# Softmax probabilities of a 256-key window packed into two key tiles, and the work moved with them

## The chip, the cores and the metric

One Trainium2 chip, one core. The metric is device time of one execution in microseconds (us), median of three runs.

## The reference, cut to what matters

Two layers over 2048 tokens of width 512 (two sequences of 1024), all in float32. Layer 0 is a linear recurrence (`W_in`, 32 decays, an associative scan, `W_out`) and a SwiGLU whose weights are rounded to three values. Layer 1 is attention with a sliding window and a mixture of experts (8 experts of width 352, two for each token, and a shared expert of width 1408). Around each of the four parts stands `x = x + layernorm(part(layernorm(x)))`. The part that the change is about:

```python
q, k = apply_rope(rms_norm(q, q_scale)), apply_rope(rms_norm(k, k_scale))   # 16 query heads, 8 key heads, width 128
mask = (j <= i) & (i - j < 256)                                # i: query, j: key
logits = where(mask, (q * ATTN_SCALE) @ k.T, finfo.min)
probs = softmax(logits)
enc = probs @ v
y = einsum('btnh,nhd->btd', enc, out_kernel)
```

The router of the experts is `logits = x @ router_weight.T`, softmax, the two largest; beside it stands a sigmoid gate of the shared expert. These ten columns are called the router products below.

## The kernel before, in words

The work is one program per engine; semaphores tie them. Each engine's order is written out by hand, call by call, and engines wait only where a call waits on a semaphore. Matrix products are made in passes of a faster float format: each operand is kept as a high and a low part (`_hi`, `_lo`), and a product is hi*hi + hi*lo + lo*hi (`passes`, L307), so nearly every value that TensorE uses is first copied to `_hi` by ACT and subtracted to `_lo` by DVE or POOL.

The phases in order of time are: the recurrence, the ternary SwiGLU (to about 430 us), attention (about 400 to 1335 us), its norm (to 1352 us), and, after a barrier, the experts (to the end). The last group of the SwiGLU overlaps the first tiles of attention, and the last head of attention overlaps the norm, whose code is `BlockNorm`.

Attention runs over 8 key heads `k` (each with 2 query heads, `GRP = 2`), and in a head over 16 tiles of 128 tokens (8 for each sequence). For a tile `j` (counted through as `m`):

- `project` (PE): 12 products into `ps_x`; `qkv_out`, `squares`, `split_v` (ACT), `rms`, `rope_add`, `split_v` (POOL), `rope` (DVE);
- `turn` (PE): 3 transposes of q and k; `split_qk` (ACT, then DVE);
- `scores` (PE, L3212): both query heads against the last `ktiles` = min(j % 8, 2) + 1 key tiles. 12 of 16 tiles have three; they are called full tiles here. Six products of 384 columns into `ps_s`;
- `row_max` (DVE, L1587): for each query head one fused instruction adds the mask, writes the masked scores to `pr` in SBUF and takes the maximum; then a tiny one (`nb`, L1597) scales it;
- `exps` (ACT, L2450): two exponentials of 384 columns in place in `pr`, with their sums; `inverse` (DVE); `weigh` (POOL, L952): two multiplications by the inverse;
- `turn_p` (PE, L3223): the probabilities are transposed, six 128x128 pieces of a full tile, into `ps_pt`, which has one buffer;
- `split_p`: `pT_hi` by ACT (L2444), `pT_lo` by DVE (L1628), 768 columns in a full tile;
- `weigh_v` (PE, L3233): nine products of 256 columns; `split_e` (ACT, DVE); `project_out` (PE): six products of 512; `sum_out` (DVE).

In the whole kernel that makes 96 full tiles, 16 with two key tiles and 16 with one. Heads 1 to 6 run the same written order; head 0 and head 7 have their own. A tile's steps are spread over some three tile times, since PE works on other tiles in between.

The norm behind attention handles each tile twice: a mean and variance (DVE), a reciprocal root (POOL), a normalization (ACT); POOL adds to x between the two halves. With `small=True` POOL makes three small instructions for each half (`_rstd_shift`, L147 to L151).

In the experts' phase, `acc` has four PSUM banks. Its PE program begins (L4336) with the router products of four blocks of 512 tokens, 8 products each; then come the shared expert's first chunks. The first weights of the shared expert (`sraw_gu`) are loaded by SP after the barrier, split by ACT and DVE.

Of the kernel before, what the change touches and what calls it, by code (L numbers as in the profile page):

```python
# [314 lines left out]
class Swiglu:  # L315
# [65 lines left out]
    def tern_op(self, dve, dst, src, w, tern_no, done):  # L381
# [159 lines left out]
NL = 10  # L541
POST_SEMS = ("y_stat", "y_rstd", "y_shift", "y_normed", "x_new", "x_stat", "x_rstd", "x_normed", "turned", "xT_hi",
# [15 lines left out]
def mixers_phase(nc, io, keep):  # L558
# [6 lines left out]
    with ExitStack() as ctx:  # L565
# [23 lines left out]
        ps_xp, ps_dd, ps_out, ps_t = ps("xp", [P, 2, BLK]), ps("dd", [P, 2, BLK]), ps("out", [P, 2, D]), ps("t", [P, 2, D])  # L589
# [16 lines left out]
        att_place = {"q_hi": 0, "q_lo": 2, "rot": 4, "pr": 8, "mask": 14, "pT_hi": 16, "pT_lo": 19, "o_lo": 22, "v_lo": 26,  # L606
# [5 lines left out]
        def aa(n, shape, dt=F32):  # L612
# [8 lines left out]
        mask = aa("mask", [P, WT * P])  # L621
# [7 lines left out]
        pr = aa("pr", [P, 2, GRP, WT * P])  # L629
        mx, nb_, sm, ri = sb("mx", [P, 2, GRP]), sb("nb", [P, 2, GRP]), sb("sm", [P, 2, GRP]), sb("ri", [P, 2, GRP])  # L630
        pT_hi, pT_lo = aa("pT_hi", [P, WT, GRP, P], F32R), aa("pT_lo", [P, WT, GRP, P], F32R)
# [3 lines left out]
        ps_pt = ps_out[:].rearrange("p a (b g t) -> p (a b) g t", b=2, g=GRP)  # L635
# [3 lines left out]
                         io["x_mid"], io["x_mid"], lambda dve, n: dve.wait_ge(sa("acc"), NT * (KVH - 1) + n + 1), tag="att_n", share=pre, small=True)  # L639

        def ktiles(i):
            return min(i % BT, WT - 1) + 1

# [18 lines left out]
        def _(sp):  # L662
# [108 lines left out]
            f.norm.tile_store(sp, 2)  # L771
            f.norm.tile_store(sp, 3)
            f.norm.tile_load(sp, 6)
            f.norm.tile_load(sp, 7)
            f.norm.tile_store(sp, 4)
            f.norm.tile_store(sp, 5)
            f.norm.tile_store(sp, 6)
            f.norm.tile_load(sp, 8)
            f.norm.tile_store(sp, 7)
            f.norm.tile_load(sp, 9)  # L780
# [3 lines left out]
            f.norm.tile_store(sp, 9)  # L784
            f.norm.tile_store(sp, 10)
            f.norm.tile_load(sp, 12)
            f.norm.tile_store(sp, 11)
            f.norm.tile_load(sp, 13)
            f.norm.tile_load(sp, 14)
            sp.wait_ge(s("down"), NT * f.groups)  # L790
# [4 lines left out]
            f.norm.tile_load(sp, 15)  # L795
# [13 lines left out]
            for n in range(NT):  # L809
                norm.tile_store(sp, n)  # L810
                if n + TPB < NT:
# [5 lines left out]
        def _(pool):  # L817
# [134 lines left out]
            def weigh(j, n):  # L952
                w = ktiles(j) * P
                pool.wait_ge(sa("ri"), n + 1)
                pool.nop(nofuse=True)
                for g in range(GRP):
                    p = pr[:, j % 2, g, WT * P - w:WT * P]
                    pool.tensor_scalar(p, p, ri[:, j % 2, g:g + 1], 1.0, ALU.mult, ALU.mult).then_inc(sa("p"), 1)  # L958

# [30 lines left out]
            f.norm.y_rstd_shift(pool, 0, (3,))  # L990
            f.norm.x_add(pool, 0, (3,), True)
            f.norm.x_rstd_shift(pool, 0, (2,))
            f.norm.x_rstd_shift(pool, 0, (3,))
            f.norm.y_rstd_shift(pool, 1, (0,))
            f.norm.x_add(pool, 1, (0,), True)
            f.norm.y_rstd_shift(pool, 1, (1,))
            f.norm.y_rstd_shift(pool, 1, (2,))
            f.norm.x_add(pool, 1, (1,), True)
            f.norm.x_add(pool, 1, (2,), True)
            f.norm.y_rstd_shift(pool, 1, (3,))  # L1000
            f.norm.x_rstd_shift(pool, 1, (0,))
            f.norm.x_add(pool, 1, (3,), True)
            f.norm.x_rstd_shift(pool, 1, (1,))
            f.norm.x_rstd_shift(pool, 1, (2,))
            f.norm.y_rstd_shift(pool, 2, (0,))
            f.norm.x_rstd_shift(pool, 1, (3,))
            f.norm.x_add(pool, 2, (0,), True)
            f.norm.y_rstd_shift(pool, 2, (1,))
            f.norm.x_add(pool, 2, (1,), True)
# [3458 lines left out]
```

## Time and profile before

| what | value |
| --- | --- |
| runs | 2028.62, 2021.69, 2028.62 us; median 2028.62 |
| profiled execution | 2022.66 us, span 2020.8 us |
| PE busy | 96% of the span, 10126 products |
| DVE, ACT, POOL busy | 73%, 59%, 40% |
| mean granted clock of TensorE | 0.989 of full speed |

Products overlap in their pipeline, so the duration of one (274 ns for a 128x128 transpose) is longer than the time from its start to the start of the next. A busy PE is not a PE at its peak; the distance between starts tells what a product costs.

### The profile page before, as it was taken

The page shows a single profiled execution, that of the slowest core. Times are in us where ns is not written, and L with a number is a line of the kernel's source. Part 1 is how long each engine was busy: PE and PEld are TensorE (multiplying, and loading weights), DVE is VectorE, ACT ScalarE, POOL GpSimd, SP SyncE. Part 2 cuts the span into 40 slices and gives each one's busy share as a digit, 9 for nine tenths or more (in the row PEclk, how much of TensorE's full clock was granted, in tenths as well). Part 3 has the DMA queues.
Part 4 walks back from the last instruction along what each step waited for, and adds up shares of the span by engine and source line. Part 5 has one row for each costly group of instructions (what it writes and reads, how often), then busy time and mean ns, then how long its engine had stood idle before and what let it go on. Part 6 is the DMA issues. An engine that isn't in the chain of part 4 may idle for free. (4 is left out here: it accounts for less than half of the span.)

```text
span 2020.8 us, 32102 instructions
## 1 busy us (share of the span) xinstructions
PE 1942.5 (96%) x10126; PEld 1649.1 (82%) x10126; DVE 1479.4 (73%) x3410; ACT 1198.0 (59%) x2977; POOL 802.0 (40%) x1202
## 2 busy tenths in 40 slices
PE   7999999989999999999999999979999999999996
PEld 5677777768888888888888888857788889887875
DVE  7788565687777777777777778966387778774665
ACT  6753222467666666666667667764386677773342
POOL 3342000685655555555555557952400000001452
PEclk9999999999999999999999999989999999999998
DMA  7344010227000000000000100234799899984563
GB/s 268 123 144 139 16 48 21 79 73 240 22 12 22 12 22 12 1 33 1 22 12 22 33 1 8 62 110 148 273 342 305 312 325 313 319 297 146 198 204 109
DMA packets 82518, 245.02 MB, mean 121 GB/s; under 512 B 10784, under 2 KB 11424, under 8 KB 80448
## 3 DMA queue, kind: packets, MB, share of 16 engines
q1 hardware_dynamic: 77232, 226.20, 32.7%
q0 software_dynamic: 5120, 16.78, 2.3%
q8 instruction: 83, 1.36, 0.3%
q14 instruction: 83, 0.68, 0.1%
HBM read 207.55 MB, written 45.61 MB: 125 GB/s over the span
## 5 line engine op out<-in xcount | busy, mean ns | idle before, releaser
L307 PE MATMUL l_xp<-att_w_hi,xT_hi 128*128 128x512 f32 x512 | 207.7, 406 | 5.1 <-ACT att_qkv L2426 4.6
L307 PE MATMUL l_xp<-att_w_hi,xT_lo 128*128 128x512 f32 x512 | 200.5, 392 | 0.0
L307 PE MATMUL l_xp<-att_w_lo,xT_hi 128*128 128x512 f32 x512 | 199.7, 390 | 0.0
L2455 ACT ACTIVATE att_pr<-att_pr,rec_nb,rec_r 128x384 f32<-128x384 f32 (+2 forms) x256 | 168.7, 662 | 36.4 <-DVE rec_nb L1597 35.6
L958 POOL TENSOR_SCALAR att_pr<-att_pr,rec_ri 128x384 f32<-128x384 f32 (+2 forms) x256 | 141.2, 564 | 122.4 <-DVE rec_ri L1626 118.8
L3885 POOL DMA_INDIRECT y<-moe_rows,moe_slotA x16 | 16.4, 1024 | 413.7 <-DMA moe_rows<-moe_lo_f 410.6
L962 POOL TENSOR_TENSOR att_rot<-att_rot,att_rot 128x384 f32<-128x384 f32 x128 | 130.0, 1016 | 107.8 <-DVE att_rot L1620 107.8
L1593 DVE CUSTOM_DVE_ANT_0 att_pr<-l_dd,att_mask 128x384 f32<-128x384 f32 (+2 forms) x256 | 119.1, 501 | 67.0 <-PE l_dd L307 60.9
L2426 ACT ACTIVATE att_qkv<-l_xp 128x512 f32<-128x512 f32 x128 | 76.4, 597 | 120.8 <-PE l_xp L307 112.1
L1631 DVE TENSOR_TENSOR att_pT_lo<-l_out,att_pT_hi 128x768 fp32r<-128x768 f32 (+2 forms) x128 | 108.8, 850 | 27.7 <-ACT att_pT_hi L2448 27.5
L2448 ACT ACTIVATE att_pT_hi<-l_out 128x768 fp32r<-128x768 f32 (+2 forms) x128 | 92.7, 724 | 41.8 <-PE l_out L3229 20.8
L307 PEld LDWEIGHTS l_xp<-att_w_hi,xT_hi 128*128 128x128 f32 x512 | 96.5, 188 | 23.9 <-issue 5.4
L2441 ACT ACTIVATE att_sq<-att_qkv 128x128 f32<-128x128 f32 x384 | 114.1, 303 | 1.3
L950 POOL TENSOR_TENSOR rec_r<-rec_ms,pre_nhalf 128x3 f32<-128x3 f32 x128 | 110.6, 864 | 10.7
L307 PEld LDWEIGHTS l_xp<-att_w_hi,xT_lo 128*128 128x128 f32 x512 | 96.2, 188 | 21.5
L307 PEld LDWEIGHTS l_xp<-att_w_lo,xT_hi 128*128 128x128 f32 x512 | 96.7, 189 | 17.4
L307 PE MATMUL l_t<-att_o_hi,att_e_hi 128*128 128x512 f32 x256 | 104.4, 408 | 1.7 <-DVE att_e_lo L1636 1.7
L307 PE MATMUL l_t<-att_pT_hi,att_v_hi 128*128 128x256 f32 x336 | 101.1, 301 | 0.8 <-DVE att_pT_lo L1631 0.6
L3229 PE MATMUL l_out<-ident,att_pr 128*128 128x128 f32 x672 | 95.4, 274 | 6.3 <-POOL att_pr L958 2.9
L4028 DVE TENSOR_TENSOR moe_rgu_lo<-y,moe_rgu_hi 128x1408 fp32r<-128x1408 f32 x59 | 95.5, 1618 | 7.3 <-ACT moe_rgu_hi L4178 7.3
L307 PE MATMUL l_t<-att_o_lo,att_e_hi 128*128 128x512 f32 x256 | 100.5, 392 | 0.0
L307 PE MATMUL l_t<-att_o_hi,att_e_lo 128*128 128x512 f32 x256 | 100.3, 392 | 0.0
(329 smaller groups left out, 6528.6 us busy)
## 6 DMA issues: line engine op xcount, KB each, us to landing
y<-in_moe_rt SPq DMA_DIRECT2D x59, 704.0 KB, 6.5
y<-in_moe_rt SPq DMA_DIRECT2D x39, 768.0 KB, 6.5
moe_sraw_gu<-in_moe_sgu SPq DMA_DIRECT2D x44, 512.0 KB, 3.7
moe_sraw_d<-in_moe_sd SPq DMA_DIRECT2D x44, 256.0 KB, 4.4
moe_xs<-in_zeros SPq DMA_DIRECT2D x39, 256.0 KB, 6.9
moe_lo_f<-moe_xs SPq DMA_DIRECT2D x39, 256.0 KB, 6.8
moe_rows<-moe_lo_f SPq DMA_DIRECT2D x39, 256.0 KB, 6.7
att_raw_w<-in_qkv_w SPq DMA_DIRECT2D x8, 1024.0 KB, 4.8
```

The source lines that it names most:

```text
L307: mm = pe.matmul(out, lhsT, rhs, start=(i == 0), stop=(i == len(terms) - 1))
L950: pool.tensor_tensor(r[:, i % 4, :], ms[:], pre.nhalf[:, 0:3, 0], ALU.pow).then_inc(sa("r"), 1)
L958: pool.tensor_scalar(p, p, ri[:, j % 2, g:g + 1], 1.0, ALU.mult, ALU.mult).then_inc(sa("p"), 1)
L962: pool.tensor_tensor(rot[:, i % 2, :], rot[:, i % 2, :], rot2[:], ALU.add).then_inc(sa("roped"), 1)
L1593: dve.tensor_tensor_reduce(pr[:, j % 2, g, WT * P - w:WT * P], ps_s[:, g, 0:w], mask[:, WT * P - w:WT * P], 1.0, -3e38, ALU.add, ALU.max, ...
L1631: dve.tensor_tensor(pT_lo[:, 0:w, :, :], ps_pt[:, 0:w, :, :], pT_hi[:, 0:w, :, :].bitcast(F32), ALU.subtract).then_inc(sa("pT_lo"), 1)
L2426: act.activation(qkv[:, i % 2, :], ps_x, ACT.Copy).then_inc(sa("qkv"), 1)
L2441: act.activation(sq[h][:], qkv[:, i % 2, HD * h:HD * (h + 1)], ACT.Square, accum_out=ss[:, h:h + 1]) \
L2448: act.activation(pT_hi[:, 0:w, :, :], ps_pt[:, 0:w, :, :], ACT.Copy).then_inc(sa("pT_hi"), 1)
L2455: act.activation(p, p, ACT.Exp, scale=r[:, j % 4, g:g + 1], bias=nb_[:, j % 2, g:g + 1], accum_out=sm[:, j % 2, g:g + 1]).then_inc(sa("exp ...
L3229: mm = pe.transpose(ps_pt[:, u, g, :], pr[:, j % 2, g, P * (WT - w + u):P * (WT - w + u + 1)], ident[:])
L4028: dve.tensor_tensor(rgu_lo[:, p % 3, :], rraw_gu(p), rgu_hi[:, p % 3, :].bitcast(F32), ALU.subtract) \
```

## The change

In a full tile the oldest key tile counts only where key > query (in the tile) and the newest only where key <= query: the two masks complement each other. The change writes the newest tile's scores over the masked places of the oldest, so that a full tile has 256 columns of scores instead of 384 from the maximum on. After the transposes the packed piece is taken apart again with a triangle of ones (`pA` = packed * triangle, `pC` = packed - pA), and `weigh_v` has nine products as before.

```diff
 def row_max(j, m):                                   # DVE
-    wait(dve, "pturn", m - 1)
-    for g in range(GRP):
-        dve.tensor_tensor_reduce(pr[...], ps_s[:, g, 0:w], mask[...], 1.0, -3e38, ALU.add, ALU.max, mx[...])
+    last = ps_s[:, :, P * (w - 1):P * w]
+    if w == WT:
+        dve.copy_predicated(ps_s[:, :, 0:P], mask[:, 0, :]..., last).then_inc(sa("mx"), 1)
+    else:
+        dve.tensor_tensor(last, last, mask[:, 2, :]..., ALU.add).then_inc(sa("mx"), 1)
+    dve.wait_ge(sa("mx"), 2 * m + 1)
+    dve.reduce_max(mx[:, j % 2, :], ps_s[:, :, 0:packed(j) * P], AX.X).then_inc(sa("mx"), 1)
 def exps(j, m):                                      # ACT
+    wait(act, "pturn", m - 1)
-        act.activation(p, p, ACT.Exp, ...)
+        act.activation(pr[:, j % 2, g, 0:packed(j) * P], ps_s[:, g, 0:packed(j) * P], ACT.Exp, ...)
+def weigh(j, n):                                     # ACT, from tile 9 of head 0 on; POOL before
+    for g in range(GRP):
+        act.activation(p, p, ACT.Copy, scale=ri[:, j % 2, g:g + 1]).then_inc(sa("p"), 1)
 def scores(j, m):                                    # PE
-    wait(pe, "mx", GRP * m)
+    wait(pe, "exp", GRP * m)
 def turn_p(j, m):                                    # PE: packed(j) = min(ktiles(j), 2); ps_pt has two buffers
-    wait(pe, "pT_lo", m)
-    for u in range(w):
+    wait(pe, "pT_lo", m - 1)
+    for u in range(packed(j)):
+def part_a(j, m):                                    # POOL; DVE in head 0 up to tile 7
+    pool.tensor_tensor(pA[:], pT[:, :, 0, :, :], mask[:, 1, :]..., ALU.mult).then_inc(sa("parts"), 1)
+def part_c(j, n):                                    # POOL
+    pool.tensor_tensor(pC[:], pT[:, :, 0, :, :], pA[:], ALU.subtract).then_inc(sa("parts"), 1)
 def weigh_v(j, m):                                   # PE: full tile
+    parts = [(t0 - 1, pT[:, :, 1, :, :], None), (t0 - 2, pA, 1), (t0, pC, 2)]
+    for q, (kt, pp, made) in enumerate(parts):
+        if made:
+            pe.wait_ge(sa("parts"), 2 * full_steps(m) + made)
```

`part_a` and `part_c` are 128x512 each (high and low parts, two query heads); `pT`, `pA` and `pC` have one buffer. The four banks of `acc` are allocated once for both phases, and attention's `ps_out` and `ps_t` lie in them. Further:

```diff
+def router(b):                                       # PE, b = 0, 1, 2, at the end of attention
+    out = (ps_out[:, 0, :], ps_out[:, 1, :], ps_e)[b]
+    passes(pe, out[0:2 * NL, :], [...])              # 8 products
 # experts' phase, PE
-for b in range(NB):
-    passes(pe, acc[b][0:2 * NL, :], [...]).then_inc(s("ps_lg"), 1)
+passes(pe, acc[NB - 1][0:2 * NL, :], [...]).then_inc(s("ps_lg"), 1)
 # SP, behind the norm's tile_store 10
+sp.wait_ge(sa("proj"), NT * KVH)
+sp.dma_start(keep["sraw_gu"][:], io["moe_sgu"][0]).then_inc(sa("sraw"), 16)
+def first_shared():                                  # ACT, in the norm behind attention
+    act.activation(keep["sgu_hi"][:, 0, :], keep["sraw_gu"][:], ACT.Copy)
 # the norm behind attention
-norm = BlockNorm(..., small=True)
+norm = BlockNorm(...)
```

Without `small`, DVE makes the first and the last of the three small instructions of each half norm (`ve`, `sh`), and POOL only the root. Each engine's written order, from the SwiGLU's last group to the end of the norm, is a new one throughout: it has the same calls for the rest, with each `last_turn`, `project` and so on some places earlier or later. In the new last stretch `router(0)` stands behind `last_turn(1, 1)`, `router(1)` behind `last_turn(2, 0)` and `router(2)` behind `last_turn(3, 1)`. In the ternary weights' splits one semaphore increment that nothing waits on is left out.

## Rows read from the trace of the kernel before

**Rows 1.** Stretch; busy us of PE, PEld, DVE, ACT, POOL; PEclk, DMA share, GB/s.
```profile
350.00:500.00 150.00, 135.49 (x685) 112.39 (x686) 117.49 (x292) 93.56 (x249) 99.95 (x179) 0.98 0.41 132
...
600.00:1200.00 600.00, 599.20 (x3458) 528.11 (x3457) 451.80 (x1476) 406.40 (x1404) 338.87 (x533) 1.00 0.05 16
...
1310.00:1352.00 42.00, 29.37 (x163) 23.93 (x161) 34.08 (x74) 28.41 (x52) 30.67 (x63) 0.83 0.36 107
...
1361.00:2021.00 660.00, 634.36 (x3164) 540.66 (x3162) 449.56 (x567) 372.63 (x502) 109.13 (x96) 0.99 0.72 252
```

**Rows 2.** Timeline of PE in head 4: start, duration, line, operation, count.
```profile
1002.33 0.36 PE L307 MATMUL l_t<-att_pT_hi,att_v_hi 128*128 128x256 f32 x1
...
1003.49 0.38 PE L3229 MATMUL l_out<-ident,att_pr 128*128 128x128 f32 x2
...
1006.52 0.60 PE L3229 MATMUL l_out<-ident,att_pr 128*128 128x128 f32 x4
1006.87 0.47 PE L307 MATMUL l_t<-att_o_hi,att_e_hi 128*128 128x512 f32 x1
...
1008.34 0.39 PE L307 MATMUL l_xp<-att_w_hi,xT_hi 128*128 128x512 f32 x1
...
1011.07 0.49 PE L3209 MATMUL l_xp<-ident,att_rot 128*128 128x128 f32 x3
1011.31 0.42 PE L307 MATMUL l_dd<-att_k_hi,att_q_hi 128*128 128x384 f32 x1
...
1012.45 0.82 PE L3229 MATMUL l_out<-ident,att_pr 128*128 128x128 f32 x6
1013.02 0.36 PE L307 MATMUL l_t<-att_pT_hi,att_v_hi 128*128 128x256 f32 x1
```

**Rows 3.** Groups of ACT and DVE by shape, whole span: busy, mean ns, idle before.
```profile
L2455 ACT ACTIVATE att_pr<-att_pr,rec_nb,rec_r 128x384 f32<-128x384 f32 x192 | 134.2, 702 | 26.4 <-DVE rec_nb L1597 25.6
...
L2426 ACT ACTIVATE att_qkv<-l_xp 128x512 f32<-128x512 f32 x128 | 76.4, 597 | 120.8 <-PE l_xp L307 112.1 <-POOL att_v_lo L939 7.0 <-issue 1.1
...
L2455 ACT ACTIVATE att_pr<-att_pr,rec_nb,rec_r 128x256 f32<-128x256 f32 x32 | 18.9, 595 | 0.2 <-DVE rec_nb L1597 0.2
...
L1593 DVE CUSTOM_DVE_ANT_0 att_pr<-l_dd,att_mask 128x384 f32<-128x384 f32 x192 | 98.9, 552 | 53.5 <-PE l_dd L307 49.1 <-PE l_out L3229 4.3
...
L1631 DVE TENSOR_TENSOR att_pT_lo<-l_out,att_pT_hi 128x768 fp32r<-128x768 f32 x96 | 91.2, 950 | 21.9 <-ACT att_pT_hi L2448 21.8
...
L1631 DVE TENSOR_TENSOR att_pT_lo<-l_out,att_pT_hi 128x512 fp32r<-128x512 f32 x16 | 10.8, 677 | 0.0
```

**Rows 4.** Groups of POOL by shape, whole span.
```profile
L962 POOL TENSOR_TENSOR att_rot<-att_rot,att_rot 128x384 f32<-128x384 f32 x128 | 130.0, 1016 | 107.8 <-DVE att_rot L1620 107.8
L958 POOL TENSOR_SCALAR att_pr<-att_pr,rec_ri 128x384 f32<-128x384 f32 x192 | 112.2, 597 | 95.5 <-DVE rec_ri L1626 91.9 <-issue 3.6
L950 POOL TENSOR_TENSOR rec_r<-rec_ms,pre_nhalf 128x3 f32<-128x3 f32 x128 | 110.6, 864 | 10.7
...
L200 POOL TENSOR_TENSOR att_x<-att_x,y 128x512 f32<-128x512 f32 x16 | 20.6, 1287 | 0.2 <-ACT y L184 0.2
```

**Rows 5.** Timeline from the norm to the experts, PE and ACT: the router products.
```profile
1352.20 0.59 PE L307 MATMUL moe_acc<-xT_hi,rw 128*20 128x512 f32 x1 [3.15 <-PEq L40]
...
1355.25 0.40 PE L307 MATMUL moe_acc<-xT_hi,rw 128*20 128x512 f32 x1
...
1360.81 0.40 PE L307 MATMUL moe_ps_g<-xT_hi,moe_sgu_hi 128*128 128x512 f32 x1
...
1355.86 1.06 ACT L4147 ACTIVATE moe_sgu_hi<-moe_sraw_gu 128x1024 fp32r<-128x1024 f32 x1 [6.16 <-DMA moe_sraw_gu<-in_moe_sgu]
```

**Rows 6.** Rotated q and k (att_rot) alone, same stretch: PE, PEld, DVE, POOL busy.
```profile
600.00:1200.00 600.00, 42.27 (x258) 32.83 (x258) 138.53 (x510) 87.47 (x86) 1.00 0.05 16
```

**Rows 7.** Timeline in head 0: POOL and DVE at the same time.
```profile
437.66 2.58 POOL L935 TENSOR_TENSOR att_o_lo<-att_raw_o,att_o_hi 128x1024 fp32r<-128x1024 f32 x1
437.91 2.48 DVE L1613 SCALAR_TENSOR_TENSOR att_rot<-att_qkv,rec_r,att_tab 128x128 f32<-128x128 f32 x1
```

More of the change, by code:

```diff
@@ L1219, in _ @@
+            rms(10, 122)
+            rope_add(9, 121)
+            split_v(9, 121)
+            norm.x_rstd(pool, 0, (1,))
+            split_v(10, 122)
+            norm.y_rstd(pool, 0, (3,))
+            part_a(6, 118)
+            norm.x_add(pool, 0, (2,), True)
+            part_c(6, 118)
             rope_add(10, 122)
             rms(11, 123)
-            weigh(8, 120)
+            norm.y_rstd(pool, 1, (0,))
+            norm.x_rstd(pool, 0, (2,))
             split_v(11, 123)
-            norm.x_add(pool, 1, (0,), True)
@@ L1237, in _ @@
+            part_a(7, 119)
+            rms(12, 124)
+            part_c(7, 119)
+            rope_add(11, 123)
+            split_v(12, 124)
+            norm.x_rstd(pool, 0, (3,))
+            norm.y_rstd(pool, 1, (1,))
+            norm.x_add(pool, 1, (0,), True)
+            rms(13, 125)
+            rope_add(12, 124)
+            norm.y_rstd(pool, 1, (2,))
             rope_add(13, 125)
             rms(14, 126)
[L1239 removed]
             split_v(13, 125)
[L1241 removed]
@@ L3372, in _ @@
+            scores(8, 8)
             turn(9, 9)
-            turn_p(5, 5)
-            project_out(0, 4, 4)
-            scores(8, 8)
-            weigh_v(5, 5)
-            turn_p(6, 6)
+            weigh_v(6, 6)
             project_out(0, 5, 5)
-            weigh_v(6, 6)
-            turn_p(7, 7)
-            turn(10, 10)
             project(0, 12, 12)
             scores(9, 9)
+            turn(10, 10)
+            project(0, 13, 13)
+            turn_p(8, 8)
             weigh_v(7, 7)
-            turn_p(8, 8)
@@ L3386, in _ @@
-            project(0, 13, 13)
             project_out(0, 6, 6)
+            scores(10, 10)
+            turn_p(9, 9)
             turn(11, 11)
-            scores(10, 10)
             weigh_v(8, 8)
-            turn_p(9, 9)
+            project_out(0, 7, 7)
             project(0, 14, 14)
@@ L3540, in _ @@
+            turn_p(2, 114)
             project_out(6, 15, 111)
             project(7, 6, 118)
-            turn_p(2, 114)
+            weigh_v(1, 113)
+            scores(3, 115)
+            turn(4, 116)
+            project_out(7, 0, 112)
+            project(7, 7, 119)
             scores(4, 116)
-            weigh_v(1, 113)
+            turn_p(3, 115)
+            weigh_v(2, 114)
             turn(5, 117)
-            project(7, 7, 119)
-            project_out(7, 0, 112)
+            project_out(7, 1, 113)
@@ L3571, in _ @@
-            project(7, 11, 123)
-            project_out(7, 5, 117)
-            scores(9, 121)
-            turn_p(7, 119)
-            weigh_v(6, 118)
-            turn(10, 122)
-            project(7, 12, 124)
+            weigh_v(5, 117)
+            project(7, 11, 123)
+            scores(8, 120)
+            turn(9, 121)
+            project_out(7, 4, 116)
+            turn_p(7, 119)
+            project(7, 12, 124)
+            weigh_v(6, 118)
+            scores(9, 121)
+            turn(10, 122)
```

1850 lines of the change are left out of this document (986 added, 864 removed).

## The prediction

> **What bounds the kernel now.** I read the busy times by stretch first [rows 1]. From 600 to 1200 us, which is attention alone, PE is busy 599.20 of 600 us at full clock; DVE 452 (75%), ACT 406 (68%), POOL 339 (56%), DMA 0.05. But matmul records overlap, so the timeline must tell whether PE is really full [rows 2]: the reader should look at starts, not at durations. Twelve products of `project` go from 1008.34 to 1011.07, 0.227 us each; six of `project_out` from 1006.87 to 1008.34, 0.245; three transposes 0.24; six score products from 1011.31 to 1012.45, 0.19; nine of `weigh_v` 1.16. Every step starts where the last one's stream ends. So attention is bound by the number of PE's products and their columns. A head has 642 products; 3458 in 600 us make 111.4 us for a head, 6.96 for a tile.
>
> The other stages: 350 to 500 us has 14.5 us of idle PE, 1310 to 1352 us (the last tiles and the norm behind them) has 12.6 of 42, with the clock at 0.83; the experts, from 1361 on, are busy 634 of 660 us [rows 1]. What starts them earlier should arrive at the end: their PE is nearly full and the last wait of most steps is PE's own stream. The DMA share of 0.72 there leaves a doubt, which I keep in the range.
>
> The Trainium skill, "Perfetto Trace Analysis", section "Identifying the Most-Contended Engine", warns that busy matmul time does not tell how near PE is to its limit, and wants the share of weight loads. That share is 528 of 600, 88% [rows 1]; going by it, up to 12% of PE's time could be slack and the saving below could be hidden. The distances between starts say otherwise, and I go by them.
>
> **Part 1, four transposes in place of six.** From the start of six transposes to the next step is 0.57 us (1012.45 to 1013.02), of four 0.35 (1006.52 to 1006.87) [rows 2]: 0.22 us less for a full tile. Scores and `weigh_v` keep their products. 96 full tiles make 21.1 us. Heads 1 to 6 (72 tiles, 15.8 us) lie in the full stage; of heads 0 and 7, some 7 tiles lie in the stretches where PE idles anyway, so I take 1.5 off: **-19.6**.
>
> **Part 2, the other engines in attention.** For a full tile, by nearest rows [rows 3, 4]:
> ACT loses 2 x (702 - 595) = 0.21 us of exponentials. It gains two scaled copies of 256 columns: no row has them; between nothing (excluded, it is an instruction) and the 128x512 copy's 597 each; I take 0.45, below the exponential of the same width (595). Its `pT_hi` is shorter too. Net +0.7 at most: 4.7 us a tile become at most 5.4 of a new 6.8, 79%.
> DVE: two fused instructions of 552 go; a predicated copy of 256 columns and a maximum over 512 come. Neither has a row. The maximum is nearest to the 128x512 subtraction from PSUM, 677; the copy lies between half of 552 and 677. I take 0.4, so 1.1 against 1.1. `pT_lo` falls from 950 to 677. DVE stays near 75%. If both unknown ones took twice as long, DVE would gain 1.1 x 16 = 18 us in a head's 109, 90% busy, still not the bound.
> POOL loses 2 x 597 and gains `part_a` and `part_c`, each nearest to the 128x512 addition, 1287: 2.57. Over 16 tiles, 3.92 - 0.90 + 1.93 = 4.95 us a tile, 73% of 6.8.
> None is the bound by its own sum, so I cost them at nothing; the cover is PE's stream, and if it were gone they would cost 2 us and more a full tile.
>
> **Part 3, new waits.** `weigh_v` now waits in its middle for `pA` and before its last three products for `pC`. `pT` has one buffer, so from the end of one tile's `weigh_v` run `pT_hi` (0.6), `pT_lo` (0.68), `part_a` and `part_c` (2.57) and four handovers of about 0.1: 4.3 us, due 0.7 to 0.8 us into the next `weigh_v` (six of nine products). In the loop's written order the least PE work between two of full tiles is before tile 11: four transposes, `project_out`, `turn`, `scores`, `project_out`: 0.35 + 1.47 + 0.24 + 1.14 + 1.47 = 4.7 us. The others have a `project` (2.73) and a `project_out` at least, 5.1 to 6 and more. Slack is 1.1 us at the tightest, 1.6 to 2.4 elsewhere; what may stand before the parts in POOL's queue is `rope_add` (1016) or `rms` (864 and a small one). `scores` now waits for the exponentials and not for the maximum: between `scores` of 12 and 13 stand `weigh_v`, `turn_p`, `project_out`, `turn`: 3.2 us, and the way through maximum (1.1), `nb`, `pT_hi` of tile 11 (ahead on ACT) and two exponentials (1.2) is about 3.5. That is 0.3 us in a head. Against that, `turn_p` loses its wait for `pT_lo` of the tile before. Bounds: 0 and 1 us a full tile; I take 0.02: **+2**.
>
> **Part 4, the router products.** The 32 products in front of the experts take 1352.20 to 1360.81, 8.6 us. Eight remain: at the same pace, 1352.20 to 1355.25, 3.05 us (the first ones at half clock). The first shared products need `sgu_lo`. Now its high part only starts at 1355.86, when the DMA has landed [rows 5]. With load and high part done before the barrier, only DVE's subtraction stands before it (128x1024, twice 677 ns), and ends before 1355. **-5.6**. The 24 moved products take 24 x 0.23 = 5.5 us at full clock, 9 at the pace of the first eight (3 x 3.05), in a stretch where PE idles 12.6 us. The second and third lie between two `last_turn`s whose gap is smaller than 1.8 us, so they can hold a turn up. Bounds 0 and 9; I take **+1.5**. The high part's copy on ACT adds about 1 us of work in the norm, the SP queue gets one load and one wait behind store 10, ahead of the load of tile 14: **+0.5**.
>
> **Part 5, the norm and head 0.** DVE takes two small instructions for each of 32 half norms from POOL, while POOL gets head 7's parts. In the last stretch POOL is busy 30.7 of 42 us and DVE 34.1 [rows 1], so relief of the one loads the other: 0, bounds -4 and +4. In head 0 the order is new and POOL's load is later and larger: 0, bounds -5 and +4. The increment left out: nothing, no one waits on it.
>
> **Sum**: -19.6 + 2 - 5.6 + 1.5 + 0.5 = -21.2 us. Against the profiled execution, 2022.66 us, that is 2001.5. The runs' median, 2028.62, stands 6 us above it and the lowest run 1 us below; I predict 2002 and let the range take the 6 us in. A measurement tells about 0.5% from no change: the border of faster is 2018.5.
>
> **Rivals.**
> **Slower: the parts set the pace.* Place: the wait on `parts` inside `weigh_v`. If `rope_add` and `rms` stand before both parts (1.0 + 1.1 us) and DVE's queue adds 0.5, the chain is 6.9 us against 5.4 to 6.2 of cover: 0.7 to 1.5 us a full tile, take 0.8: +77 - 21, 2078. It decides from about 0.33 us a full tile on (32 us for the 21 gained and 10 more). Against it: no tile's neighbours are all this tight, and the order puts the parts mostly back to back. Chance 0.06.
> *The shared port.* While POOL subtracts `o_lo` from 437.66 to 440.24, a DVE instruction of 128x128 with two SBUF sources takes 2.48 us and ends 0.15 behind it [rows 7]: DVE was held to POOL's end. DVE's instructions of this kind are those of `rope`, 138.5 us in 86 tiles, 1.6 each [rows 6], and `nb`. POOL would have 4.95 us of a tile, together 6.6 to 6.8 of 6.8. If the two excluded each other wholly, there would be no slack; queues on both sides would give back all of part 1, a time near 2020. For it: the row. Against it: the probable exclusion is shorter, as DVE's other work has a PSUM source, and the row shows it for one pair only. Chance 0.07.
> The Trainium skill, "SBUF — State Buffer", section "Who interferes with whom", has this as a rule: a DVE instruction with two SBUF inputs contends with a GpSimd instruction that reads SBUF, and one with at most one SBUF input doesn't. It speaks against this change, which puts 2.6 us of such reads on POOL; the row agrees.
> *Half of it.* Small waits of many kinds eat half of part 1: 2011 to 2013. Chance 0.13.
> *More.* Head 0 and the last stretch gain too (-5 and -4), since `turn_p` has two buffers and POOL's three-step root is gone: 1992. Chance 0.13.
> That the packing doesn't shorten `turn_p` is not possible: its loop has `packed(j)` steps.
>
> **How the numbers follow.** The forecast (1997 to 2008, by the bounds of parts 3 to 5 and the median's 6 us) has 0.61. Faster: 0.61 + 0.13 + 0.13, and 0.01 of the port's 0.07; same: its other 0.06; slower: 0.06. The range, 1989 to 2018, holds the forecast and the cases of more and of half; the port's and the parts' are left out.
>
> **What would show it.** PE: `turn_p` with 480 transposes, 10126 - 192 = 9934 products; 618 of them in a head in about 109 us; PE still above 99% between 600 and 1200. Waits of PE for POOL's `att_pA` or `att_pC` near nothing. The first shared product about 3 us behind the first router product of the experts. Wrong would be: waits of PE on POOL above 0.2 us a full tile, DVE's `nb` and `rope` much longer than now, or a longer stretch from the last score product to the barrier.

## The result, and the profile after

Four runs of the changed kernel have a median of 2090.17 us (2086.72 to 2092.78) against 2027.11 us for the kernel before: a ratio of 1.0316, 95% interval [1.03, 1.0332]. The change makes the kernel 3.2% slower. I had forecast 2002 us, with 0.06 for slower.

The profiled execution took 2088.52 us, its span is 2086.7 us. The page's busy times, then the busy times by stretch: all engines in attention, and `att_rot` (the rotated q and k) alone; they answer to [rows 1, 6].

```profile
PE 1953.5 (94%) x9934; PEld 1641.7 (79%) x9934; DVE 1626.8 (78%) x3224; ACT 1241.6 (59%) x3215; POOL 899.0 (43%) x1086
...
600.00:1200.00 600.00, 567.90 (x3140) 488.17 (x3141) 523.88 (x1228) 413.34 (x1482) 393.18 (x463) 0.99 0.05 16
```
```profile
600.00:1200.00 600.00, 40.70 (x246) 29.92 (x246) 229.49 (x489) 84.14 (x81) 0.99 0.05 16
```

9934 products are the ones that I counted. But in 600 us only 3140 run: a head has 618, so it takes 118.1 us (111.4 before, 108.8 forecast), and PE idles 32 us. There are 81.3 tiles in the stretch. DVE is busy 6.44 us of each (5.24 before), ACT 5.08, POOL 4.84. The surprise is in the second fence: `rope`'s six DVE instructions take 229.49 / 489 x 6 = 2.82 us a tile, 1.63 before. (This is time in which at least one of them runs. Their records overlap a little; added up they are 3.2 us, the figure that some expectations below use.) The change doesn't touch them.

The groups by shape in the whole span (as [rows 3, 4]). `pA`, `pC`, the scaled copy (`att_pr`) and the maximum (`rec_mx`) are what the change added; `att_rot` is `rope` on DVE:

```profile
L979 POOL TENSOR_TENSOR att_pC<-att_pT,att_pA 128x512 fp32r<-128x512 f32 x96 | 126.7, 1320 | 8.8 <-DVE att_pA L1688 4.1
...
L974 POOL TENSOR_TENSOR att_pA<-att_pT,att_mask 128x512 fp32r<-128x512 f32 x90 | 119.9, 1332 | 85.5 <-DVE att_pT L1683 85.4
...
L1665 DVE SCALAR_TENSOR_TENSOR att_rot<-att_qkv,rec_r,att_tab 128x128 f32<-128x128 f32 x128 | 111.3, 870 | 0.0
...
L1669 DVE SCALAR_TENSOR_TENSOR att_rot<-att_qkv,rec_r,att_tab 128x64 f32<-128x64 f32 x256 | 101.3, 396 | 0.0
...
L2541 ACT ACTIVATE att_pr<-att_pr,rec_ri 128x256 f32<-128x256 f32 x210 | 95.5, 507 | 55.4 <-DVE rec_ri L1678 54.8
...
L1663 DVE TENSOR_TENSOR att_rot<-att_qkv,att_tab 128x256 f32<-128x256 f32 x128 | 93.7, 732 | 17.5 <-POOL rec_r L963 16.9 <-issue 0.6
...
L1647 DVE TENSOR_REDUCE rec_mx<-l_dd 128x2 f32<-128x512 f32 x112 | 77.4, 691 | 3.8
```

The added work costs nearly what I took. `rope` is what grew: a 128x128 instruction takes 870 ns on average, which alone takes 350. The timeline at the change from head 4 to head 5 (heads and tiles count from 0) shows why. One idle time of PE, with what led to it (DVE, POOL and ACT around `rope`; the starts are the first column):

```profile
997.32 0.45 DVE L1663 TENSOR_TENSOR att_rot<-att_qkv,att_tab 128x256 f32<-128x256 f32 x1
...
997.44 1.49 POOL L974 TENSOR_TENSOR att_pA<-att_pT,att_mask 128x512 fp32r<-128x512 f32 x1
...
997.69 1.39 DVE L1665 SCALAR_TENSOR_TENSOR att_rot<-att_qkv,rec_r,att_tab 128x128 f32<-128x128 f32 x1
...
999.00 1.38 DVE L1669 SCALAR_TENSOR_TENSOR att_rot<-att_qkv,rec_r,att_tab 128x64 f32<-128x64 f32 x1
...
999.01 1.29 POOL L979 TENSOR_TENSOR att_pC<-att_pT,att_pA 128x512 fp32r<-128x512 f32 x1
...
1000.26 1.27 POOL L939 TENSOR_TENSOR att_w_lo<-att_raw_w,att_w_hi 128x512 fp32r<-128x512 f32 x1
...
1000.31 1.37 DVE L1672 TENSOR_TENSOR att_rot<-att_qkv,att_tab 128x128 f32<-128x128 f32 x1
...
1002.20 0.15 DVE L1678 RECIPROCAL rec_ri<-rec_sm 128x2 f32<-128x2 f32 x1
...
1002.39 0.91 ACT L2541 ACTIVATE att_pr<-att_pr,rec_ri 128x256 f32<-128x256 f32 x2 [3.24 <-DVE rec_ri L1678]
...
1003.35 0.33 PE L3375 MATMUL acc<-ident,att_pr 128*128 128x128 f32 x1 [2.37 <-ACT att_pr L2541]
```

Read the ends: DVE's 997.69 + 1.39 is 999.08, POOL's `pA` ends at 998.93; 1000.38 and 1000.30; 1001.68 and 1001.53. Three DVE instructions in a row each last until 0.08 to 0.15 us behind the end of a POOL instruction. Two of these are the parts; the third is a weight split (`att_w_lo`) that POOL had before the change too. That delays the reciprocal behind them, ACT's scaled copies wait 3.24 us for it, and PE waits 2.37 us for them. Behind the idle time the granted clock falls to its lower level for a while: products of `project` that start 0.23 us apart at 1004.75 are 0.43 apart from 1005.29 on. The stretch from 1003 to 1009 us has a mean of 0.72 (PEclk, the third number from the end):

```profile
1003.00:1009.00 6.00, 5.21 (x17) 4.08 (x18) 4.67 (x10) 2.36 (x7) 2.05 (x2) 0.72 0.50 176
```

The waits of PE from 600 to 1200 us (us in total, times, longest) name the same chain, and nothing of `pA` or `pC`:

```profile
PE acc L3375 <- ACT att_pr L2541: 18.2, 10, 2.4
PE l_dd L307 <- DVE att_k_lo L1633: 5.3, 10, 0.7
PE l_xp L3356 <- DVE att_k_lo L1633: 5.0, 6, 0.8
```

Nearly half of PE's idle time in that stretch (14 of 31 us in stops of over 0.3 us) lies, as here, between a head's last `project` and the next head's first.

I matched all DVE and POOL instructions from 520 to 1240 us by time. DVE instructions with a source in PSUM last the same beside POOL's parts as alone (all within 0.01 us on average). Those with two SBUF sources are held when they start while a part runs, or within 0.01 us before it: 24 of 128x128 beside `pA` are each 1.03 to 1.05 us longer than the shortest of their kind, 18 of 128x64 beside `pC` 1.10 to 1.12 us, and 31 of 128x256 beside `pA` 0.37 to 1.12 us, by how much of the part was left. Who starts first matters: 24 of 128x256 that started 0.09 to 0.16 us before `pA` are at most 0.05 us longer, and there POOL's `pA` takes 1.39 to 1.49 us, where 27 that meet no such DVE instruction take 1.27 to 1.30.

Where the 65.9 us between the two spans lie: the landmarks are the first and last start of `project`'s products and the first of the shared expert's, before and after (lines of the tiles' instructions; first and last start stand behind the durations):

```profile
L307 PE MATMUL l_xp<-att_w_hi,xT_hi x512: 387/393/776, 405.0 to 1297.4; 128*128 128x512 f32 x171
L307 PE MATMUL moe_ps_g<-xT_hi,moe_sgu_hi x176: 393/396/496, 1360.8 to 1995.3; 128*128 128x512 f32 x176
```
```profile
L307 PE MATMUL l_xp<-att_w_hi,xT_hi x512: 387/390/775, 407.4 to 1350.6; 128*128 128x512 f32 x171
L307 PE MATMUL moe_ps_g<-xT_hi,sgu_hi x176: 391/396/484, 1425.0 to 2061.0; 128*128 128x512 f32 x176
```

Attention (first to last `project`) goes from 892.4 to 943.2 us, +50.8. The last stretch (to the first shared product) goes from 63.4 to 74.4, +11.0. The start is 2.4 later, and the experts take 661.7 against 660.0.

### The profile page after: what moved, and what is told of

It is laid out like the page before. It is cut to its first block and busy times, and to the rows that moved or that the text cites. A ratio compares the mean times of both kernels' runs of the same rounds, so it can differ in the third digit from the quotient of the medians.

```text
span 2086.7 us, 31545 instructions
## 1 busy us (share of the span) xinstructions
PE 1953.5 (94%) x9934; PEld 1641.7 (79%) x9934; DVE 1626.8 (78%) x3224; ACT 1241.6 (59%) x3215; POOL 899.0 (43%) x1086
## 3 DMA queue, kind: packets, MB, share of 16 engines
q8 instruction: 81, 1.33, 0.3%
## 5 line engine op out<-in xcount | busy, mean ns | idle before, releaser
L2553 ACT ACTIVATE att_pr<-l_dd,rec_nb,rec_r 128x256 f32<-128x256 f32 (+1 forms) x256 | 138.7, 549 | 77.3 <-DVE rec_nb L1649 77.1
L974 POOL TENSOR_TENSOR att_pA<-att_pT,att_mask 128x512 fp32r<-128x512 f32 x90 | 119.9, 1332 | 85.5 <-DVE att_pT L1683 85.4
L2541 ACT ACTIVATE att_pr<-att_pr,rec_ri 128x256 f32<-128x256 f32 x238 | 105.2, 494 | 59.2 <-DVE rec_ri L1678 58.6
L979 POOL TENSOR_TENSOR att_pC<-att_pT,att_pA 128x512 fp32r<-128x512 f32 x96 | 126.7, 1320 | 8.8 <-DVE att_pA L1688 4.1
L307 PE MATMUL acc<-att_o_hi,att_e_hi 128*128 128x512 f32 x256 | 109.6, 428 | 14.3 <-DVE att_e_lo L1693 10.7
L1665 DVE SCALAR_TENSOR_TENSOR att_rot<-att_qkv,rec_r,att_tab 128x128 f32<-128x128 f32 x128 | 111.3, 870 | 0.0
L1663 DVE TENSOR_TENSOR att_rot<-att_qkv,att_tab 128x256 f32<-128x256 f32 x128 | 93.7, 732 | 17.5 <-POOL rec_r L963 16.9
L307 PE MATMUL acc<-att_o_hi,att_e_lo 128*128 128x512 f32 x256 | 103.2, 403 | 0.0
L307 PE MATMUL acc<-att_o_lo,att_e_hi 128*128 128x512 f32 x256 | 102.9, 402 | 0.0
L307 PE MATMUL l_dd<-att_k_hi,att_q_hi 128*128 128x384 f32 (+2 forms) x256 | 87.7, 342 | 14.8 <-DVE att_k_lo L1633 9.9
```

Source lines behind the costliest of these rows:

```text
L307: mm = pe.matmul(out, lhsT, rhs, start=(i == 0), stop=(i == len(terms) - 1))
L974: pool.tensor_tensor(pA[:], pT[:, :, 0, :, :].bitcast(F32), mask[:, 1, :].unsqueeze(1).unsqueeze(1) .broadcast_to([P, 2, GRP, P]), ALU.mul ...
L979: pool.tensor_tensor(pC[:], pT[:, :, 0, :, :].bitcast(F32), pA[:].bitcast(F32), ALU.subtract) \
L1663: dve.tensor_tensor(rq, q, tab(0, 0)[:, t, :].unsqueeze(1).broadcast_to([P, GRP, HD]), ALU.mult) \
L1665: dve.scalar_tensor_tensor(out=rot[:, i % 2, GRP * HD:3 * HD], in0=kx, scalar=rk, in1=tab(1, 0)[:, t, :], op0=ALU.mult, op1=ALU.mult).then ...
L2541: act.activation(p, p, ACT.Copy, scale=ri[:, j % 2, g:g + 1]).then_inc(sa("p"), 1)
```

## The experiments

"Changed" is the changed kernel. Each kernel was timed beside the kernel before, whose medians then were 2024.3 to 2026.7 us, so small differences are best read from the ratios. `rope` is DVE's `att_rot` time of a tile, from 600 to 1200 us, and "attention" is first to last `project` in the profiled execution. The kernels without parts or with fills leave the taking apart of the packed piece out, so their outputs are not attention's; they are used for their times alone.

**Do the parts cost, and is it POOL's time or its reads?**

Changed kernel without parts:
```diff
 def part_a / part_c:
+    pass
 # weigh_v
-    parts = [(t0 - 1, pT[:, :, 1], None), (t0 - 2, pA, 1), (t0, pC, 2)]
+    parts = [(t0 - 1, pT[:, :, 1], None), (t0 - 2, pT[:, :, 0], None), (t0, pT[:, :, 0], None)]
```


> Leaves out part_a and part_c; weigh_v multiplies the packed piece with both key tiles and waits for no parts. Before is about 2027 us, the change 2090. Port theory (DVE's instructions with two SBUF sources are held by POOL's part_a and part_c): rope falls from about 3.2 us a tile to 1.7 and the time to 2000-2010, as the sum of the prediction had it. Rival 1 (length of the chain through the parts inside weigh_v): also about 2005. Rival 2 (exponentials holding ps_s, division on ACT, a written order made for other costs): it stays above 2050.

2022.05 us, ratio 0.9995 [0.9984, 1.0005]; attention 880.9 us, `rope` 1.60. `rope` came out as the port has it, the time did not: 12 us above my 2000 to 2010.

Parts that only write:
```diff
-    pool.tensor_tensor(pA[:], pT..., mask..., ALU.mult)
+    for i, part in enumerate((pA[:, 0, 0, :], pA[:], pA[:])):
+        pool.memset(part, 0.5)                        # part_c in the same way; same places and waits
```


> part_a and part_c become fills of the same two tiles that only write SBUF (three each, about 1.3 us in all), with the same waits before and behind them; the packed piece is not taken apart. Port theory: DVE's rope and nb are no longer held, 1.7 us of rope a tile, time 2000-2015. Chain theory (latency of the parts and POOL's load): nothing changes, 2080-2100.

2014.53 us, ratio 0.995 [0.9934, 0.9967]; attention 872.3 us. Busy times as above (all, then `att_rot` alone), and `rope` beside a part:

```profile
600.00:1200.00 600.00, 599.12 (x3400) 525.51 (x3399) 446.38 (x1331) 450.68 (x1616) 412.25 (x764) 1.00 0.05 16
```
```profile
600.00:1200.00 600.00, 43.24 (x265) 32.95 (x264) 130.26 (x524) 89.28 (x88) 1.00 0.05 16
```
```profile
714.98 0.41 DVE L1665 TENSOR_TENSOR att_rot<-att_qkv,att_tab 128x256 f32<-128x256 f32 x1
...
715.05 1.37 POOL L977 MEMSET att_pA<- 128x128 f32 x3 [0.78 <-DVE att_pT L1685]
...
715.30 0.35 DVE L1667 SCALAR_TENSOR_TENSOR att_rot<-att_qkv,rec_r,att_tab 128x128 f32<-128x128 f32 x1
```

POOL is busier than in the changed kernel (412 us against 393), its parts are as long (1.37 us) and are waited for by the same instructions. Yet DVE runs through them (0.41 and 0.35 us), `rope` takes 1.49 us, PE has no wait in the stretch and a head takes 600 / (3400 / 618) = 109.1 us. So what costs is that the parts read SBUF: 943.2 - 872.3 = 71 us of attention. And without it, part 1 of the forecast is all there in attention: 892.4 - 872.3 = 20.1 us. It doesn't all reach the end: the span is only 5.2 us shorter than before, since attention starts 2.1 us later, the last stretch is 6.6 us longer (70.0) and the experts take 666.2 us against 660.0. (This profiled execution, 2017.67 us, is the slowest of its four, so some of that is scatter.)

The Trainium skill, "SBUF — State Buffer", section "Who interferes with whom", says that a DVE instruction with two SBUF inputs contends with a GpSimd instruction that reads SBUF, and not with one that only writes it. These two kernels show both halves of it.

Both parts on DVE (the same two instructions, behind `split_p` of the tile before, none on POOL):

> Both part_a and part_c of every full tile on DVE, right behind its split_p; POOL has none. Port theory: rope is free again (1.7 us a tile), but DVE gets 1.5 us of its own a full tile and stands at some 6.5 us of a 6.8 us tile: 2030-2060, between the two kernels. Chain theory: the chain is 1.1 us shorter, so below 2030.

2067.3 us, ratio 1.0217 [1.02, 1.0234]; attention 915.1 us, `rope` 1.56, DVE 509 of 600 us. That is above my 2030 to 2060. The hold is gone; what DVE's busy time shows in its place is its own added work.

**Is the router's part worth what I said?** Kernel before, with the router products, the load behind store 10 and `first_shared` as in the diff:

> The kernel before with the router part alone: three blocks' router products in the last stretch, first shared weights loaded and copied there. Prediction's parts 4: 5.6 us less behind the barrier, about 2 us more before it: 2023 against 2027. Rival (the moved products hold the norm's transposes up): 2027 or more.

2024.19 us, ratio 0.9996 [0.9985, 1.0007]. The last phase begins like this (PE's timeline, as [rows 5]):

```profile
1356.37 0.59 PE L307 MATMUL acc<-xT_hi,rw 128*20 128x512 f32 x1 [3.34 <-PEq L40]
...
1359.74 0.63 PE L307 MATMUL moe_ps_g<-xT_hi,sgu_hi 128*128 128x512 f32 x1
```

Eight products take 3.4 us, but they start at 1356.37 where 32 started at 1352.20. The first shared product is 1.1 us earlier than before (1360.8), and from it to the span's end (2021.9) are 662.2 us, not 660.0. The part is worth nothing that can be told from no change (the interval reaches 0.15% below it).

**The reads alone, in the old order.** Kernel before, with two idle POOL instructions behind `weigh` of each full tile of heads 1 to 6:
```diff
+    pool.tensor_tensor(x[:, 0, :], x[:, 1, :], x[:, 2, :], ALU.add)    # first kernel: 1302 ns, reads
+    pool.memset(x[:, 0:3, :], 0.5)                                      # second: 1382 ns, only writes
```


> The kernel before with two idle additions of 128x512 on POOL (two SBUF sources, 1.29 us each) behind the division of each full tile in heads 1 to 6, 144 in all; nobody waits for them but POOL's own queue. POOL's busy time per tile rises by 1.9 us to 84%. Port theory: DVE's rope goes from 1.6 to 2.5-3.3 us a tile, PE starts to idle, 2050-2100. Rival (the cost in the changed kernel was the chain or POOL's load, the port is minor): under 2040, and the same as the fills of the next run.

> As the run before, but each idle instruction is one fill of 128x1536, about 1.3 us, that reads nothing. Port theory: rope stays at 1.6 us a tile; what is left is POOL's own load of 84%: 2025-2040, clearly below the additions. Rival: equal to the additions.

2142.02 us with reads (1.0579 [1.0561, 1.0597]), 2135.23 with fills (1.0548 [1.0531, 1.0566]). Both forecasts of the port were misses: 2050 to 2100 with 2.5 to 3.3 us of `rope` for the reads, 2025 to 2040 for the fills. By the times alone this pair would say that reading costs 7 us, and the rest is POOL's queue. The waits of DVE from 600 to 1200 us, reads first, then fills:

```profile
DVE att_rot L1640 <- POOL rec_r L951: 75.8, 34, 4.2
```
```profile
DVE att_rot L1640 <- POOL rec_r L951: 114.2, 39, 4.5
```

In this order `rms` stands behind the idle pair in POOL's queue, and `rope` waits for it. With fills `rope` keeps its 1.65 us and DVE stands in this wait instead; with reads it takes 1.96. An engine at 56% of its time has no room for 2.6 us at that place, whatever they do. So the 71 us above are the price of the reads in the changed kernel's order, and a price read in one order isn't the price in another.

**Can `rope` be moved away?** Changed kernel, heads 1 to 6: twelve `rope` moved ahead of the `split_p` that releases the parts, two `rms` ahead of `part_a`:

> The changed kernel, heads 1 to 6: on DVE the 12 ropes that stood up to five calls behind the split of a full tile (that is beside POOL's two part instructions) go ahead of that split; two rms on POOL go ahead of a part_a. No work is added or left out. Port theory: rope falls from 3.2 to under 2.3 us a tile there, time 2045-2075 against 2090. Rival (order and other waits make the cost): 2090 or more, as the split comes 1.6 us later.

2139.36 us, ratio 1.0561. `rope` falls to 1.61 us as expected, and the time rises by 49 us: now `part_a` waits for `split_p` 125.6 us (66.4 before the move), ACT's scaled copies for the reciprocal 84.7 and `rope` for `rms` 59.3, and PE waits 9.8 us for `pC`. The time is a miss (2045 to 2075 expected), and a warning: holds gone, order lost. This run moves two things at once, so it neither proves the port nor speaks against it.

**The norm's small instructions.** Changed kernel with `small=True`, and then the kernel with fills with it:

> The changed kernel with the norm behind attention as in the kernel before: POOL makes all three small instructions of a half norm, DVE none. If the 11 us that the stretch from the last projection to the first shared product got longer come from DVE's added instructions: 2082. If from the port and the parts in head 7: 2090 or more, as POOL's queue gets 20 us more.

> Both parts as fills, as in the earlier run of 2014.5, and the norm behind attention with small=True, which puts two of its three small instructions from DVE back on POOL; the same leaving out as in that run (pA and pC hold a constant). If the norm's instructions on DVE cost by themselves what they did in the changed kernel (7 us): 2007.5 within 2, last project to last router product 7 us shorter. If they only cost there because POOL's parts held DVE: 2013 to 2016.

2083.27 us (1.0285 [1.0268, 1.0302]; changed: 1.0316 [1.03, 1.0332]), and 2020.71 us (0.9967 [0.9957, 0.9978]; fills alone: 0.995 [0.9934, 0.9967]). Each pair of intervals touches, so neither step is clear of noise: by the ratios the small instructions on POOL are some 6 us better with POOL's reads in place, and some 3 us worse with fills. Neither of my two expectations for the second held. The traces agree in direction only. With the reads, 2.1 us of the gain lie in the last stretch and 0.4 in attention. With fills, attention is 878.4 - 872.3 = 6.1 us longer, behind 1200 us, in head 7, where POOL is busy 84 of 110 us between 1250 and 1360 (69 without them). Nor do these instructions explain the last stretch: it takes 72.3 us with `small=True`, 70.0 with fills, 72.2 with both and 71.1 with no parts at all, against 74.4 changed and 63.4 before.

**One part at a time.** `part_c` as fills; `part_a` as fills; `part_a` on DVE with `part_c` on POOL:

> Only part_c is made of three fills (1.37 us, no read of SBUF); part_a stays as in the changed kernel (pC is filled with a constant, so its product with v isn't attention's). Port: of the time that DVE is held between 520 and 1240 us of the changed kernel, some 73 us lie over pC and 41 over pA, so 64% goes; of the 71 us that separate the changed kernel's attention from that with fills alone, 46 come back: 2090 - 46 = 2044, within 10, rope (att_rot on DVE) 2.0 to 2.2 us a tile. Rival, only the length of POOL's queue counts: POOL is as busy as before, so 2090 within 5. Rival, any one hold is enough to break the order written for free engines: above 2065.

> The other half: part_a is made of three fills, part_c reads pT and pA as in the changed kernel (so both pieces differ from attention's). Port, by the same shares: 36% of the holds go, 25 of the 71 us come back: 2065 within 10, rope 2.3 to 2.5 us a tile. POOL's queue alone: 2090 within 5. Any hold is enough: above 2080. If the costs of the two add up, the gains of this run and of the one with part_c filled make 71 to 76 us together; clearly less would mean that each alone already pays most of it, clearly more that they only hurt together.

> part_a is made by DVE (one instruction of 128x512, two SBUF sources, behind split_p) in every full tile, part_c stays on POOL. DVE gains some 0.7 us of its own work a full tile and loses the holds over pA, 0.5; the holds over pC stay, and part_a itself, with two SBUF sources, can be held as well. Port: about as slow as the changed kernel, 2080 to 2095. Rival, the chain of parts on POOL's queue is what hurts (both parts 2.64 us, now 1.3 on POOL and 0.7 on DVE): 2060 to 2070.

2025.48 us (0.9989 [0.9976, 1.0002]); 2037.11 us (1.0051 [1.0034, 1.0068]); 2061.47 us (1.0169 [1.0146, 1.0193]). For the first I had expected 2034 to 2054 and `rope` of 2.0 to 2.2 us, for the second 2055 to 2075 and 2.3 to 2.5: both came out far better, since I had shared the 71 us out by the time of the holds. Filling one part gains 65 us, filling the other 53, filling both 76. The prices don't add up: one reading part alone costs 11 (`pA`) or 23 us (`pC`) over fills, the two together 76 (8, 20 and 74 by the ratios). The holds don't add up either: `rope` goes from 1.49 us (fills) to 1.93 with reads by `pA` alone, 1.83 by `pC` alone and 2.82 by both. 0.44 and 0.34 us a tile make 0.78; together they are 1.33. Two reads back to back catch one instruction of the same `rope` after the other, as in the timeline above: from 600 to 1200 us, 51 of 81 `rope`s have two or more instructions that are over 0.15 us longer than their shortest, but only 6 of 87 with `pC` filled and 5 of 85 with `pA` filled. Over 128 tiles that is 170 us of `rope`, and 76 reach the end; for `pC` alone it is 23 of 44, for `pA` alone 11 of 56. PE's busy time (`part_c` filled, then `part_a` filled) shows how little the first costs:

```profile
600.00:1200.00 600.00, 595.88 (x3379) 522.41 (x3378) 476.85 (x1324) 450.16 (x1610) 418.30 (x628) 1.00 0.05 16
```
```profile
600.00:1200.00 600.00, 586.88 (x3319) 512.59 (x3318) 479.19 (x1302) 439.65 (x1570) 410.25 (x614) 1.00 0.05 16
```

The third has, with the four pieces below (their intervals overlap), the lowest time of the packed kernels with all of the computation. The port's forecast for it, 2080 to 2095, was too high; its rival's, by the length of the parts' chain on POOL, was 2060 to 2070 and held. The likely reason is that I had taken `pC`'s holds at what they are behind `pA`'s. This run by itself doesn't tell the two apart; the fills do.

**The length of a hold.** Parts cut into 2 instructions of 128x256, into 4 of 128x128, and `part_a` on DVE with `part_c` in 2:
```diff
+    for h in range(2):
+        pool.tensor_tensor(pA[:, h], pT[:, h, 0], mask..., ALU.mult)      # for 4: also over g
```


> part_a and part_c are cut in two instructions of 128x256 each (high and low half), on POOL as before; the same values come out. One POOL piece should take 0.75 us (128x384 takes 1.03, 128x512 1.32), so POOL gains 0.36 us a full tile, and a held DVE instruction waits 0.7 at most in place of 1.3. Long hold: an instruction of DVE gets in between the pieces, each held one loses half, rope falls from 2.8 to 2.1 to 2.3 us a tile, time 2045 to 2065. Total reading: rope stays at 2.7 or more, and POOL's longer queue makes it 2090 to 2105. Rival on the gap: POOL's next piece is queued so closely that DVE is held until both are done; then also no gain, 2090 or more.

> Each part in four instructions of 128x128, which should take 0.48 us each (the 128x128 subtraction on POOL takes 0.49): both parts 3.9 us a full tile in place of 2.65, 15 us more POOL in a head, POOL 76% of a head of 118 at the least. Long hold: a held instruction waits 0.4; rope 1.9 to 2.1 us a tile, but the parts arrive 1.2 us later, which the slack of 1.1 to 2.4 us behind them nearly uses up: 2050 to 2080. Total reading: above 2110.

> part_a on DVE in every full tile as in the run of 2061.5, part_c on POOL in two pieces. Long hold: rope falls from 2.12 to 1.8 to 1.9 us a tile and part_a on DVE is held less, 2045 to 2055; not below the kernel before (2026), since DVE's own 0.7 us a tile stays. Total reading: 2061 to 2070.

2070.72 us (1.0224 [1.0207, 1.0241]), 2063.22 us (1.0179 [1.0162, 1.0196]), 2072.52 us (1.0226 [1.0209, 1.0243]); `rope` 2.76, 2.28 and 2.13 us. The timeline of four pieces:

```profile
711.91 1.95 POOL L976 TENSOR_TENSOR att_pA<-att_pT,att_mask 128x128 fp32r<-128x128 f32 x4 [0.56 <-DVE att_pT L1687]
...
712.61 0.47 DVE L1667 TENSOR_TENSOR att_rot<-att_qkv,att_tab 128x256 f32<-128x256 f32 x1
...
713.00 0.54 DVE L1669 SCALAR_TENSOR_TENSOR att_rot<-att_qkv,rec_r,att_tab 128x128 f32<-128x128 f32 x1
...
713.46 0.48 DVE L1673 SCALAR_TENSOR_TENSOR att_rot<-att_qkv,rec_r,att_tab 128x64 f32<-128x64 f32 x1
```

DVE gets one instruction in for each piece of POOL (0.49 us), whatever its own size: 128x128 and 128x64 both last a piece. So shorter holds come in larger number: with two pieces 37 of 82 `rope`s have four or five held instructions, with four pieces 57 of 84 have four or more (5 of 81 uncut). Two pieces leave `rope` as it was, though the time falls by 20 us; four take half a microsecond off it, at 75 us more of POOL in 600. I had expected 2.1 to 2.3 and 1.9 to 2.1 us of `rope`, and 2045 to 2065 and 2050 to 2080 us: of these four only the last held. That two pieces gain 20 us with `rope` unchanged isn't explained. For the third kernel cutting is a loss of 11 us (2045 to 2055 and 1.8 to 1.9 us of `rope` expected), which I can't explain from its rows: `rope` is the same, and POOL's `pC` takes 1.61 us for 1.34.

All of them, in one table:

| kernel | median us | ratio | attention us | `rope` us a tile |
| --- | --- | --- | --- | --- |
| before | 2027.11 | 1 | 892.4 | 1.63 |
| before, router part | 2024.19 | 0.9996 | 892.3 | 1.63 |
| changed | 2090.17 | 1.0316 | 943.2 | 2.82 |
| both parts as fills | 2014.53 | 0.995 | 872.3 | 1.49 |
| both as fills, `small=True` | 2020.71 | 0.9967 | 878.4 | 1.49 |
| no parts | 2022.05 | 0.9995 | 880.9 | 1.60 |
| `pC` as fills | 2025.48 | 0.9989 | 881.5 | 1.93 |
| `pA` as fills | 2037.11 | 1.0051 | 891.4 | 1.83 |
| `pA` on DVE | 2061.47 | 1.0169 | 915.4 | 2.12 |
| four pieces | 2063.22 | 1.0179 | 915.8 | 2.28 |
| both on DVE | 2067.3 | 1.0217 | 915.1 | 1.56 |
| two pieces | 2070.72 | 1.0224 | 926.2 | 2.76 |
| `pA` on DVE, `pC` in two | 2072.52 | 1.0226 | 923.2 | 2.13 |
| changed, `small=True` | 2083.27 | 1.0285 | 942.8 | 2.80 |
| changed, `rope` ahead | 2139.36 | 1.0561 | 994.2 | 1.61 |
| before, idle fills | 2135.23 | 1.0548 | 1000.8 | 1.65 |
| before, idle reads | 2142.02 | 1.0579 | 1006.8 | 1.96 |

No packed kernel that computes all is faster than the kernel before. What fills reach, 0.5% below it, is the most that was seen of this packing.

## Why the prediction was wrong

**What failed** is one sentence of part 2: "None is the bound by its own sum, so I cost them at nothing". The sums were right: POOL 4.84 us a tile (4.95 forecast), ACT 5.08 (5.4 at most), DVE's new pair 0.42 + 0.69 us (1.1). But POOL's 2.65 us of reads aren't only POOL's time. They are DVE's too, wherever `rope` or `nb` falls beside them. DVE's busy time rose to 6.44 us a tile of 7.4, and it stands in one order: a late `rope` makes a late reciprocal. Reads in place of fills cost 71 us of attention.

**The rival "the shared port"** had the mechanism, the row and the place, and a chance of 0.07 at 2020. Its price failed. I wrote that it "would give back all of part 1", as if the loss ended where the gain did. Nothing limits it so: DVE's hold is work in a queue, and it cost over three times what part 1 gives (71 us against 20.1). I should have priced it as I did the parts' rival: [rows 7] show a hold up to the end of POOL's instruction; with two of 1.29 us per full tile and six instructions of `rope` behind one another, a bound of 2 x 1.3 us a full tile was there to be worked out, up to 250 us in 96. Against it I said that the exclusion is "shorter, as DVE's other work has a PSUM source". DVE's PSUM sources are indeed never held, as the matched instructions show, but `split_p` releases `part_a` and stands right ahead of `rope` in many places, so the two meet.

**Part 1**, -19.6: right. The kernel with fills has 20.1 us less attention and 109.1 us a head. In the changed kernel four transposes take 0.35 us, as forecast (as [rows 2], which by the count of `project`s lie at the start of head 5; nothing hangs on the number):

```profile
1013.00 0.60 PE L3375 MATMUL acc<-ident,att_pr 128*128 128x128 f32 x4
1013.35 0.36 PE L3391 MATMUL acc<-att_pT,att_v_hi 128*128 128x256 f32 x1
```

**Part 3**, +2: right for `weigh_v` (no wait of PE for `pA` or `pC` in the stretch). "The parts set the pace" is refuted by fills of equal length.

**Part 4**, -5.6 + 1.5 + 0.5: the first term held, the second failed, and the sum doesn't reach the end. In the router kernel the products before the shared expert's take 3.4 us in place of 8.6: -5.2. But the first of them starts 4.2 us later, where I had 2.0 for the moved products and the SP queue, and the last `project` starts only 0.3 us later. So of the 12.6 us of idle PE that I counted as cover, little can have lain at the places where they stand. That makes 1.1 us less to the first shared product, and the experts take 2.2 more, which no row explains.

**Part 5**, 0 with bounds of 4 us: the last stretch grew by 11.0 us, where with part 4 I had it 3.6 shorter. Without any part it is 71.1 us, against 62.0 in the router kernel, so some 9 us belong neither to the parts nor to the router. `small=True` takes 2 off beside the reading parts and adds 2 beside fills. The rest must lie in the new written order of the end of attention or in the packing's other waits there. That wasn't separated and stays open. So does why no parts at all (2022.05) is slower than fills (2014.53).

**Without the reads** the forecast would still have missed: the kernel with fills took 2014.5 us, inside the range but 12 us above 2002, as half or more of the 20.1 us of part 1 was lost again outside attention. I had costed those places at nothing or as a gain.

The range's upper end, 2018, left out the port with the parts. What I named as the sign of being wrong, "DVE's `nb` and `rope` much longer than now", is what came.

## What to carry to other kernels

Before giving POOL work that reads SBUF, list DVE's instructions with two SBUF sources that can run beside it, and price the overlap as DVE's time, up to the whole of POOL's instruction each; then follow DVE's queue to what it releases. A loss of this kind isn't capped by the gain of the change. A fill of equal length in the same place tells a port from a queue in one run.

## What the runs showed of the hardware

- A DVE instruction with two SBUF sources that starts with or during a part of POOL (1.3 us, reads SBUF) ends just behind it, the later the larger it is: 0.02 us for 128x2, 0.08 for 128x64, 0.15 for 128x128, 0.28 for 128x256. One that started 0.09 to 0.16 us before the part isn't held; POOL's part is 0.1 to 0.2 us longer there. In pieces of 0.49 us DVE gets one instruction in for each piece.
- Not every POOL read holds: beside the power of 128x3 (869 ns, which reads two SBUF tiles) `nb` was never longer (37 instructions, 0.00 us on average), while beside `rope_add` it was 0.35 us longer (18). The rule of the Trainium skill ("SBUF — State Buffer", section "Who interferes with whom") makes no such exception; here the measurement decides.
- Fills of 1.37 us beside `rope`: no class of `rope`'s instructions is longer than its median by 0.01 us on average (72 of 128x64 beside `pC`'s fills, 0.00 us).
- A predicated copy of 128x256 in PSUM takes 423 ns, a maximum over 128x512 from PSUM 691 ns, a scaled copy of 128x256 in SBUF on ACT 507 ns.
